# The last layer's experts: eight dense experts replaced by 15 sorted blocks of 128 rows

## What is computed

```
scores = xt @ gate_w.T                       # 8 experts
top_vals, top_idx = top_k(scores, 2)
top_w = softmax(top_vals)
combine = einsum('tke,tk->te', one_hot(top_idx, 8), top_w)
h  = silu(einsum('td,ehd->eth', xt, w1)) * einsum('td,ehd->eth', xt, w3)     # 128 -> 512
ye = einsum('eth,edh->etd', h, w2)                                           # 512 -> 128
y  = einsum('te,etd->td', combine, ye)
x  = layernorm(x + y)
```

## Time and profile before

| | us |
|---|---|
| median of 3 runs (4170.47 to 4176.15) | 4173.82 |
| the profiled execution, its own time | 4180.67 |
| its span (first to last instruction) | 4179.0 |
| PE matmul busy | 3893.9 (93%) |
| DVE busy | 2766.9 (66%) |
| ACT busy | 1978.4 (47%) |
| POOL busy | 948.6 (23%) |
| DMA traffic | 91.87 MB, 22 GB/s mean |

### The profile page before, as it was taken

The page is one execution under the profiler, slowest core; times in us unless marked ns, Lnnn a source line. Parts: engine busy times, 40 slices in busy tenths (PEclk is TensorE's granted clock), DMA queues, the critical chain, the costliest instruction groups (busy, mean ns, idle before and its releaser), DMA issues. The chain is left out here.

```text
span 4179.0 us, 70765 instructions
## 1 busy us (share of the span) xinstructions
PE 3893.9 (93%) x23508; PEld 2394.3 (57%) x23508; DVE 2766.9 (66%) x8036; ACT 1978.4 (47%) x5740; POOL 948.6 (23%) x1040
## 2 busy tenths in 40 slices
PE   7999899999999999999989998999999999999998
PEld 4644455665655655666646444565556556555665
DVE  3787767677767747664447886776777776476644
ACT  1732445655555533663228224555565555346722
POOL 0145332233322200000001462322323321000000
PEclk8999999999999999999979999999999999999999
DMA  1100000000000010000010000000000000201000
GB/s 57 43 17 1 17 7 18 24 17 24 17 24 2 26 58 21 31 37 9 4 59 6 17 1 17 7 17 24 18 24 17 24 2 26 72 7 56 12 9 11
DMA packets 15853, 91.87 MB, mean 22 GB/s; under 512 B 2176, under 2 KB 8064, under 8 KB 12032
## 3 DMA queue, kind: packets, MB, share of 16 engines
q1 hardware_dynamic: 15488, 87.27, 5.8%
HBM read 86.22 MB, written 1.05 MB: 21 GB/s over the span
## 5 line engine op out<-in xcount | busy, mean ns | idle before, releaser
L610 PE MATMUL ps_O<-wide,V 128*64 128x256 f32 (+4 forms) x5152 | 596.2, 393 | 1.9 <-ACT wide L638 1.9
L691 ACT ACTIVATE EX<-NB,neg 128x154 f32<-128x154 f32 (+3 forms) x768 | 402.7, 531 | 107.6 <-DVE neg L719 107.6
L561 PE MATMUL ps_S<-KT,QT 64*128 64x154 f32 (+7 forms) x1936 | 373.5, 456 | 59.9 <-POOL QT L1619 25.3
L656 POOL COPY RX<-recips 128x256 f32<-128x256 f32 (+2 forms) x356 | 156.6, 440 | 1127.9 <-DVE recips L734 1127.9
L745 DVE TENSOR_TENSOR QT<-ps_O,RS 128x512 f32<-128x512 f32 x212 | 146.5, 691 | 395.2 <-PE ps_O L610 394.6
L640 DVE COPY wide<-ps_P 128x512 f32<-128x512 f32 (+4 forms) x528 | 339.8, 647 | 75.2 <-PE ps_P L592 72.4
L610 PEld LDWEIGHTS ps_O<-wide,V 128*64 128x64 f32 (+4 forms) x5152 | 266.8, 127 | 194.6 <-issue 110.7
L429 POOL TENSOR_TENSOR small<-small 128x4 f32<-128x4 f32 x112 | 113.6, 1014 | 1065.6 <-DVE small L414 902.8
L561 PE MATMUL ps_T<-KT,QT 64*128 64x154 f32 (+5 forms) x968 | 322.2, 435 | 3.4 <-ACT EX L691 3.4
L561 PE MATMUL ps_OUT<-KT,QT 64*128 64x154 f32 (+5 forms) x968 | 325.2, 434 | 0.1
L592 PE MATMUL ps_P<-consts,EX 128*128 128x128 f32 (+1 forms) x1956 | 294.1, 286 | 25.9 <-ACT RS L647 13.0
(11 more groups left out here) (388 smaller groups left out, 8231.5 us busy)
## 6 DMA issues: line engine op xcount, KB each, us to landing
weights<-in_w_dram SPq DMA_DIRECT2D x10, 1664.0 KB, 6.9
weights<-in_w_dram SPq DMA_DIRECT2D x2, 6148.0 KB, 17.5
weights<-in_w5next_dram SPq DMA_DIRECT2D x6, 1664.0 KB, 6.9
weights<-in_w_dram SPq DMA_DIRECT2D x2, 4200.0 KB, 12.9
weights<-in_reltab_dram SPq DMA_DIRECT2D x2, 4096.0 KB, 14.1
weights<-in_w_dram SPq DMA_DIRECT2D x8, 640.0 KB, 3.9
weights<-in_w_dram SPq DMA_DIRECT2D x5, 832.0 KB, 4.5
weights<-in_w_dram SPq DMA_DIRECT2D x2, 2050.0 KB, 7.9
```

Of the source, the lines that this page charges most:

```text
L561: ins = pe.matmul(S4[k][:, a * N:(a + 1) * N], QT[strip, c, qts[a] * P:(qts[a] + 1) * P], self.keys(c)[strip, 0:N], start=True, stop=True)
L610: ins = pe.matmul(O1[self.slot * j:self.slot * (j + 1), q0 * P:(q0 + self.nq) * P], self.value(c * self.hpc + j, kc), self.probs(rd, j)[:, ...
L656: pool.tensor_copy(RX[:, q0 * P:(q0 + self.nq) * P].rearrange("p (n s) -> p n s", s=self.slot), of.unsqueeze(2).broadcast_to([P, self.nq * ...
L691: ins = act.activation(ex[:, a * N:(a + 1) * N], src, ACT.Exp, bias=neg[:, at:at + 1], scale=-1.0 if self.added else 1.0, accum_out=sums[: ...
```

## The change

**Compute.** Swiglu becomes a class of its own. DVE ranks the experts per token as before, and a small matmul with a triangle of ones (`count`) gives each of the 1024 (token, choice) pairs its place among the pairs of its expert. Each expert's pairs are padded to whole blocks of 128 rows; 15 blocks are always enough. POOL scatters the rows of X by 8 indirect DMAs of 128 rows each into a DRAM buffer `sorted` (`sort`), SP loads the buffer back as 15 tiles (`sync_blocks`), and PE turns the tiles (`turn_blocks`) and ACT copies them to XST. For block i, PE reads the block's expert (times 512) from SBUF into a register and multiplies the block with 512 columns of w1 and of w3, taken from the register's place; ACT and DVE form the hidden rows (128 tokens x 512) as before; PE transposes them in four pieces, ACT copies them, and PE multiplies with the four chunks of w2, again from the register's place. DVE copies the answer to Y, SP writes Y in four DMAs to a DRAM buffer `answers`, POOL gathers it by 8 indirect DMAs (`fetch`), and DVE adds the two rows of each token with their weights (8 instructions in `tail`).

**Places.** Lane 0's gate, ranks, places and scatter run inside L3Cross lane 1 (list `late` with G after round 1 and F after round 3, `choose` at i == 2, `place` at i == 4, the scatters in POOL's rounds 5 to 7). Lane 1's run inside lane 0's Swiglu (gate at i == 3, count at i == 5 on PE; logits and choose at i == 4, counts and place at i == 6 on DVE). Lane 0's `tail` runs at i == 10 and 11 of lane 1. Lane 1's fetch and tail have no step behind them. The idle matmuls of the old stage are gone. Once at the start, 2 x 960 KB of zeros are written to the sorted buffers; between the iterations POOL resets its DMA semaphores.

```diff
+        class Swiglu(LaneStep):
+            E = 8
+            out_n = BLOCKS
...
+            def count(self, pe, bank):
+                pe.wait_ge(self.r.mixed, 1)
+                pe.matmul(bank[:, 0:32], upto[:, :], self.both, start=True, stop=False)
+                pe.matmul(bank[:, 0:32], every[:, :], self.before[:, 0:32], start=False, stop=True)
+                pe.matmul(bank[:, 32:40], every[:, :], self.before[:, 32:40], start=True, stop=True
+                          ).then_inc(self.r.recip, 1)
...
+            def sort(self, pool, lo, hi):
...
+                for k in range(lo, hi):
+                    pool.indirect_dma_start(xs[self.n][:, :], bass.IndirectOffsetOnAxis(self.L.slots[:, k:k + 1], 0),
+                                            self.L.X[:, k % NT, :], None).then_inc(s_sorted[self.n], 16)
+            def sync_blocks(self, sp):
+                sp.wait_ge(s_sorted[self.n], 128)
+                sp.dma_start(self.XS.rearrange("p (j d) -> p j d", d=P),
+                             xs[self.n][:, :].rearrange("(j p) d -> p j d", p=P)).then_inc(s_blocks[self.n], 16)
+            def sync_answers(self, sp):
...
+                for lo in range(0, BLOCKS, 4):
+                    hi = min(lo + 4, BLOCKS)
+                    sp.wait_ge(self.r.hid_dve, hi)
+                    sp.dma_start(ys[self.n][lo * P:hi * P, :].rearrange("(j p) d -> p j d", p=P),
...
+            def fetch(self, pool):
+                pool.wait_ge(s_answers[self.n], 64)
+                for k in range(2 * NT):
+                    pool.indirect_dma_start(self.got[:, k * P:(k + 1) * P], None, ys[self.n][:, :],
...
+            def pe(self, pe):
...
+                for i in range(BLOCKS + 2):
+                    if i < BLOCKS:
+                        where.append(at)
+                        pe.wait_ge(r.evac_act, i // 4 + 1)
+                        if i >= 2:
+                            pe.wait_ge(r.hid_sb, i - 1)
+                        for m, name in enumerate(("w1", "w3")):
+                            pe.matmul(RING[2 * (i % 2) + m][:, :], self.XST[:, i * P:(i + 1) * P],
+                                      self.w(name)[:, bass.ds(at, 512)], start=True, stop=True).then_inc(r.part, 1)
+                        if i + 1 < BLOCKS:
+                            at = pe.value_load(self.L.experts[0:1, i + 1:i + 2], min_val=0, max_val=3584)
...
+                        for c in range(4):
+                            ins = pe.transpose(S[j % 2][:, c * P:(c + 1) * P], QT[:, 2 + j % 2, c * P:(c + 1) * P], ident)
...
+                        for c in range(4):
+                            ins = pe.matmul(OUT[:, (j % 4) * P:(j % 4 + 1) * P], QT[:, 4 + j % 2, c * P:(c + 1) * P],
+                                            self.w("w2")[:, c * P:3584 + (c + 1) * P][:, bass.ds(where[j], P)],
+                                            start=(c == 0), stop=(c == 3))
...
+            def tail(self, dve, n):
+                if n == 0:
+                    dve.wait_ge(s_fetched[self.n], 128)
+                    dve.wait_ge(r.act_step, 1)
+                    for k in range(2 * NT):
+                        t = k % NT
+                        ch.inc(dve.scalar_tensor_tensor(Z[:, t, :], self.got[:, k * P:(k + 1) * P], self.share[:, k:k + 1],
+                                                        Z[:, t, :] if k >= NT else L.X[:, t, :], ALU.mult, ALU.add))
...
         class L3Cross(LaneStep):
-                                     added=lambda h, qt: L.padb[:, min(qt, 2), :], exes=[EX[:, e, :] for e in range(4)])
+                                     added=lambda h, qt: L.padb[:, min(qt, 2), :], exes=[EX[:, e, :] for e in range(4)],
+                                     late={1: ["G"], 3: ["F"]} if L is lanes[1] else None)
...
-                self.att.pool(pool, self.r)
+                sort = {5: (0, 3), 6: (3, 6), 7: (6, 8)} if self.att.late else {}
+                self.att.pool(pool, self.r, beside=lambda i: self.nxt.sort(pool, *sort[i]) if i in sort else None)
...
+                sp.wait_ge(s_boot3, 6)
+                for n in range(2):
+                    sp.dma_start(xs[n][:, :].rearrange("(j p) d -> p j d", p=P),
+                                 wide[:, 0:SLOTS].rearrange("p (j d) -> p j d", d=P)).then_inc(s_boot4, 16)
+                sp.wait_ge(s_boot4, 32)
```

More of the change, by code:

```diff
@@ L22 @@
 RSQRT8 = 8.0 ** -0.5
+BLOCKS = 15
+SLOTS = BLOCKS * P
 WEIGHTS = {
@@ L232, in build @@
         picked = sb("picked", [P, NT, 640])
+        upto, every = sb("upto", [P, P]), sb("every", [P, P])
+        counting = sb("counting", [P, 20])
+        xs = [nc.dram_tensor(f"sorted{n}", (SLOTS, P), F32, kind="Internal").ap() for n in range(2)]
+        ys = [nc.dram_tensor(f"answers{n}", (SLOTS, P), F32, kind="Internal").ap() for n in range(2)]
         flatZ = Z[:, :, :].rearrange("p t d -> p (t d)")
@@ L276, in build @@
         s_store = pair_sem("store")
+        s_blocks = [pair_sem(f"blocks{n}") for n in range(2)]
+        s_answers = [pair_sem(f"answers{n}") for n in range(2)]
         def C(name, c=0, n=1, parts=P):
@@ L1749, in pe @@
                     ins = pe.matmul(TB[:, t * E:(t + 1) * E], L.XT[:, t * P:(t + 1) * P],
-                                    w("gate" if self.swiglu else "wr"), start=True, stop=True)
+                                    w("wr"), start=True, stop=True)
                 ins.then_inc(r.gate, 1)
@@ L1914, in dve @@
-                self.weigh(dve)
-                for e in range(2, self.E):
-                    self.add(dve, e - 2)
-                    self.products(dve, e, 0, 4)
-                self.add(dve, self.E - 2)
+                for i in range(BLOCKS + 2):
+                    if i < BLOCKS:
+                        dve.wait_ge(r.ready, i + 1)
+                        dve.wait_ge(r.part, 2 * i + 2)
+                        if i >= 2:
+                            dve.wait_ge(r.probsT, i - 1)
+                        dve.tensor_tensor(QT[:, 2 + i % 2, :], RING[2 * (i % 2) + 1][:, :], QT[:, i % 2, :], ALU.mult
+                                          ).then_inc(r.hid_sb, 1)
+                    if i >= 2:
+                        j = i - 2
+                        dve.wait_ge(r.out, j + 1)
+                        dve.tensor_copy(self.Y[:, j * P:(j + 1) * P], OUT[:, (j % 4) * P:(j % 4 + 1) * P]
+                                        ).then_inc(r.hid_dve, 1)
+                    if n == 0:
+                        if i < 2:
+                            self.beside(dve, i)
+                        if i == 4:
+                            self.nxt.logits(dve, TB)
+                            self.nxt.choose(dve)
+                        if i == 6:
+                            self.nxt.counts(dve, TB)
+                            self.nxt.place(dve)
+                    elif i in (10, 11):
+                        self.beside(dve, i - 10)
@@ L2257, in pool, with late_pe, late_dve, beside_dve @@
                 self.fresh(pool)
-                self.att.pool(pool, self.r)
+                sort = {5: (0, 3), 6: (3, 6), 7: (6, 8)} if self.att.late else {}
+                self.att.pool(pool, self.r, beside=lambda i: self.nxt.sort(pool, *sort[i]) if i in sort else None)
+            def late_pe(self, pe, j):
+                bank = self.att.late_bank(j)
+                self.nxt.gate(pe, bank) if j == "G" else self.nxt.count(pe, bank)
+            def late_dve(self, dve, j):
+                bank = self.att.late_bank(j)
+                self.nxt.logits(dve, bank) if j == "G" else self.nxt.counts(dve, bank)
+            def beside_dve(self, dve, i):
+                if i == 2:
+                    self.nxt.choose(dve)
+                if i == 4:
+                    self.nxt.place(dve)
             def pe(self, pe):
@@ L2287, in dve @@
                 dve.wait_ge(s_pad_cut, 4)
-                self.att.dve(dve, r)
+                if self.att.late:
+                    self.att.dve(dve, r, beside=lambda i: self.beside_dve(dve, i), late=self.late_dve)
+                else:
+                    self.att.dve(dve, r)
                 ch.link(dve.tensor_tensor(Z[:, :, :], self.L.X[:, :, :], row4(R_("L3x_bo")), ALU.add))
@@ L2401, in _ @@
                     sp.sem_clear(range(min(pair_sems), max(pair_sems) + 1))
+                @block.gpsimd
+                def _(pool):
+                    of = range(soft[0].num, soft[3].num + 1)
+                    pool.dma_reset(of)
+                    pool.sem_clear(of)
 def pack(np, parts, widths):
```

294 lines of the change are left out of this document (206 added, 88 removed).

## The result

| | before | after |
|---|---|---|
| median of four runs, us | 4173.3 (4170.5 to 4176.2) | 4059.7 (4052.2 to 4063.6) |
| ratio, with its 95% interval | | 0.9725 (0.9711 to 0.974) |
| profiled execution, its own time | 4180.67 | 4062.76 |
| span | 4179.0 | 4061.1 |

The change makes the kernel 113.7 us faster. The forecast was 4091, 31 us too high; its range (4050 to 4145) held the result, and the rival in which the issue is free, 4064, lies 4 us from it.

A forecast was written before the change was run, and what follows sets the result against it. PE's work bounds Swiglu: stage 181 to 97.5 us, issue +13.5, choose stall +3, seams +1.4, L3Cross +6.3, end +14.8 give -44.5 an iteration, -83 with the start. Forecast 4091 us, range 4050 to 4145.

The forecast's parts named there:

- the rival in which the issue is free: Swiglu on PE: issue costs nothing, so 2 x 13.5 = 27 us go too, giving 4064; chance 0.12.
- The bound and PE's work: Swiglu is bound by PE's work; a block needs 3.05 us, the stage goes from 181 to 97.5 us an iteration.
- the issue term: Swiglu blocks on PE: instruction issue takes 0.45 us beyond the array's 3.05, adding 13.5 us an iteration.
- The waits for XST: Swiglu lane starts: PE waits half a microsecond a lane for the first copy, 1.0; ACT's table loads add 0.7 a lane.
- Register loads and address rows: PE's sequencer per block: 32 instructions 1.76 us, eight address rows 1.2, load 0.5; sums to 3.5 us against 3.05.
- L3Cross: L3Cross lane 1: choose costs 3 us, place 2, gate and count matmuls 1.3; 6.3 us more an iteration.
- Lane 0's way through memory: Scatters between POOL's last spreads, then the sorted-row load, covered by the last round and projection; cost nothing.
- Lane 1's end: Behind lane 1's last block: copy, answers' DMA, eight gathers, landing and sums, less the old sum; 14.8 us an iteration.
- Start: Start of the kernel: 1.9 MB of zeros behind the first DMAs on the same queue; 6 us, once.
- The sequencer-bound case: Swiglu on PE: the sequencer can't run ahead past address rows; 4.4 us a block, 54 us more, 4145; chance 0.15.
- About 3 us each: Scatters and gathers on POOL go one after the other at this cost; 46 us more, 4137; chance 0.10.
- A register load that drains PE: Swiglu on PE: each load leaves the array idle for 3.1 us; 159 us more, 4250; chance 0.06.

The follow-up runs named there:

- e1: Changed kernel with no register: block i always takes the columns of expert i//2, so no loads or matmul address rows; 4058.2 us, ratio 0.9717.
- e2: Changed kernel with four more register loads of the same word behind each load, 224 in all; 4136.9 us, ratio 0.99.
- e10: Changed kernel with the ranks computed twice on DVE in the attention of lane 1, same result; 4068.6 us, ratio 0.9754.
- e6: Changed kernel with lane 0's eight scatters behind the attention's last spread instead of between the last four; 4071.7 us, ratio 0.9762.
- e4: Changed kernel with the start-up zeros issued on ACT's queue from another buffer, not waited for before the third stage; 4058.0 us, ratio 0.9728.
- e5: Changed kernel with two more register loads of the same word behind each load, 112 in all; 4067.9 us, ratio 0.9756.
- e7: Changed kernel with the expert's w1 and w3 copied to fixed tiles by ACT and DVE, and no transposes of hidden rows; 4053.5 us, ratio 0.9718.
- e9: On e7 plus e4 and a shorter last tail: three PSUM banks, DVE's work in pieces, lane 1's count and place one block later; 4043.7 us, 0.9692.
- e11: Changed kernel computing only the first 12 of 15 blocks in each lane, so the output differs; 4030.5 us, ratio 0.9663.
- e12: On e9, with lane 1's x, gate, count, choose and place each one block earlier in lane 0; 4042.7 us, ratio 0.9692.

## Why the prediction was right, and where it was off

**The bound and PE's work: right.** The steady block is 3.05 us. Without the issue term I had 97.5 + 3 + 1.4 = 101.9 us for the stage, and it is 101.8. That the two agree to 0.1 us is partly luck, since items inside were off both ways. The waits for XST (1.0) and for ACT's tables (1.4) are not there: in front of the first blocks PE has no idle time over 0.1 us that ends with ACT. A table load takes ACT 1.28 us; at the seam the sigmoid's is at 1964.72, before the sorted rows are turned, and silu's at 1969.59, behind the first copies to XST (1968.00) and not in front of them. `choose` stalls PE for 0.95 us (L1896 at 1935.29), not 3. Instead some 4 us stand where the lanes begin and end, which I had not counted: the last two w2 rows of a lane, for one, are 1.63 and 1.73 us behind the row before, where their work is 1.33 and 0.89.

**Register loads and address rows: the step that failed.** "3.5 us, 0.45 above the array's 3.05" a block, 27 us in all, is 0 in the steady blocks (e1) and 2.3 us in all where the lanes begin and end. Of the three prices the load was nearly right: 0.5 and its two rows, 0.8, taken, 0.66 measured. The instruction and the address row were not: 32 at 0.055 and the other six rows at 0.15 make 2.7 us, and e2 shows 1.15 for all but the load. A transpose's two instructions in 0.11 us are the array's pace, not the sequencer's (1.15 us for 32 of them and six rows is 0.036 at most for one), and rows that issue DMAs on SP are no measure of an address row on PE (its row shows 46 ns, the gap behind it not counted). I had written that these were bounds from above and still put the forecast almost on them.

**L3Cross: the mechanism right, the size off.** 6.3 us were taken; 2.9 and 4.4 came. `choose` adds 8.06 - 5.53 = 2.5 to its round (3 taken), and the two rounds with `place` 12.03 - 11.06 = 1.0 (2 and 1.3 taken for it and PE's small matmuls). The round behind runs in 4.85 us, 0.7 less than the 5.53 it had been held to. The 1.5 us that iteration 2 takes more are the clock. PE stands for DVE at L1896 in both, 1.63 and 1.65 us; in the first the granted clock stays at 1.00, in the second it is 0.50 from 3896.6 to 3900.0, and the next round takes 7.04 us (3896.98 to 3904.02) instead of 5.47:

```profile
3896.04 0.41 PE L1896 MATMUL ps_P<-XR,upto 128*128 128x32 f32 x2 [1.65 <-DVE wide L655]
```

```profile
3897.00:3900.00 3.00, 3.00 (x20) 2.69 (x21) 2.42 (x16) 1.16 (x5) 0.00 (x0) 0.50 0.00 0
```

The prediction had no term for that. Twelve of the traces have this wait unchanged (all of the changed kernel and its variants but e10), two times each: behind 20 of the 24 the clock fell and the attention took 58.1 us or more (59.7 in three), behind four it did not and it took 56.5.

**Lane 0's way through memory: right.** It costs nothing, and e6 shows how much cover there is: there the load of the sorted rows is issued 0.5 us ahead of the projection's last row (1911.98 to 1912.5) instead of 12.8 (1901.59 to 1914.4), 12.3 later, and PE waits 4.8, so some 7 us are cover. The changed kernel's own trace says the same: its rows land at 1907.28 and are first read at 1914.48. The 1.01 us of the earlier trace rows is not POOL's cheapest row, as I had it: its copies of 128x256 take 0.40. A scatter takes 0.98.

**Lane 1's end: right.** 14.8 taken, 15.1 and 15.2 measured. The gathers stand 1.26 us apart, not 1.1, and the sums start 2.4 us behind the last one's start. PE is idle for 27.8 us between the iterations.

**Start: right, a little less.** 6 taken, 4.1 at the first transposes and 5.4 at the landmark of the table; 3 of it comes back in e4.

**The sum.** Issue -27, L3Cross -5.3, the untouched stages -2.6, the start -0.6, the ends +0.7 and the rows behind the last store -0.1 make up the 35 us between -83 and -117.9.

**The rivals.** "PE waits for nothing in issue" is what happened. The sequencer-bound case is real and 1.24 us a block away: e2 stands in it. "About 3 us each" for scatters and gathers did not happen: they take 0.98 and 0.96 us of POOL, and the gathers that ran beside DVE's products and copies, lane 0's at 1970.53 to 1979.35, take 0.95 to 1.00 each. A register load that drains PE did not happen either: a block with one load has no idle time in its 3.05 us, and two more cost it 0.12 (e5). Nor did the waits on the address rows hold the sequencer back in the steady blocks, where it is 1.7 us ahead.

## What to carry to other kernels

Price the sequencer by what it does alone, not by rows in which the array or a DMA sets the pace: here, by difference, 32 instructions and six address rows take 1.15 us together, and a register load 0.66 (e2), beside an array that needs 3.05 a block. When a stage gets shorter, list what it was covering: every step here that shortened lane 0 or its pipeline (e7, e9, e11) met the next wait within 1 to 3 us and gave part of the gain back. The best kernels found are e12 at 4042.7 us and e9 at 4043.7, with the same ratio, 0.9692; most of what they have over the changed kernel's 4059.7 comes from the copied weights, the start and the shorter last tail.

## What the runs showed that I had not expected

- **A wait of PE can cost more than its length, and did not cost the same each time.** Behind idle times of 2.38 us (e11), 2.58 and 2.95 (e9), 3.24 (e12), 3.98 (e10) and 4.77 (e6) the granted clock fell to 0.50 for some us, and the rows behind cost 1.5 to 3 us on top. Behind shorter ones it went either way: it stayed at 1.00 behind 0.95 us (the changed kernel), 1.75 (e7), 1.84 (e11) and 2.20 (e2), fell behind one of e7's two waits of 1.42, and behind most of the 1.64 us at L1896. So no single length of a wait parts the two here. DVE's stall of 1.6 us at L1896 cost that or, with 58.1 us for the attention instead of 56.5, 3.2.
- **The rows of PE's sequencer leave out the gaps.** In e2 a load shows 0.30 + 0.15 + 0.02 us and is repeated every 0.66.
- **The releaser named can be the wrong one.** In e2 PE's idle time is put down to DVE's product or, in other blocks, to issue, while it was the loads on PE's own sequencer each time.
